# Eight projection matmuls of an attention step, split four and four around the transposes of the probabilities

## The chip, the core and the metric

The kernel runs on one core of a Trainium2 chip. Its engines are TensorE (PE in the rows; its weight loads are listed apart as PEld), VectorE (DVE), ScalarE (ACT), GpSimd (POOL) and SyncE (SP). Each works through its own list of instructions, and they wait for each other on semaphores. The metric is the device time of one execution in microseconds (us); lower is better.

## What is computed

A decoder of two layers on x of 8 batches by 100 tokens by 512. The change lies in one stage of it, the grouped attention with cross attention of layer 0, cut here to what matters:

```
q  = _ln(fp8_linear(ln_out, wq))        # 16 heads of 128, in 8 groups of 2 heads
k, v = _ln(fp8_linear(ln_out, wk)), fp8_linear(ln_out, wv)     # 8 groups of 128
core = _gqa(q, k, v)                    # softmax(q k^T * scale) v, 100 x 100 per head
qx = _ln(fp8_linear(ln_out, wqx))       # a second set of queries
kx, vx = split(cond @ w_kv_x.T)         # cond: 361 rows of context per batch
xout = _gqa(qx, _ln(kx), vx)            # 100 x 361 per head
catq = _div_clamp_fp8(concatenate([core, xout]), proj_smooth)
return einsum('bsi,oi->bso', catq, wproj) * (proj_in_scale * proj_w_scale)
```

The last line is the output projection, from 4096 features to 512.

## The kernel before, in words

The program is a row of stages. The function `grouped_attention` is the one that the change touches. It runs 64 steps, one for each of 8 groups g (outer loop) and 8 batches b (inner loop), numbered n = 8g + b. One step does, for its group and batch, the projections of tokens and context and their norms, and it does the softmax and the weighing of the values for the step before it, n-1. So work of two neighbouring steps overlaps. Nothing reorders anything: each engine runs its instructions in the order in which the function for that engine writes them, and a wait on a semaphore holds all that stands behind it on that engine.

On TensorE a step is, in this order:

- `project_tokens` (L822): 48 matmuls of 100 x 256 or 100 x 128, in bf16 (weights in three parts).
- `scores(n-1)` (L858, L859): scores of the two heads into banks 6 and 7.
- `project_context` (L836): keys and values of the context, 12 matmuls in the program and 24 instructions in the profile, since each f32 matmul there shows as two.
- `turn_probs(n-1)` (L867, L870): waits for `prob_ready`, the normalised probabilities, and transposes them in eight matmuls against the identity. The last one raises `pt_mm`.
- `project_out` (L893), from step 6 on: eight matmuls of 128 x 400 (four rows j by the high and the low part of the weights), all added up in bank 4. They belong to an older unit, six steps back, and their inputs have long been made. The last one raises `proj_mm`.
- `weigh_values(n-1)` (L877, L879): waits for the copies `pT` of the transposed probabilities, then four matmuls in the program.
- `turn(n)` (L845, L849): transposes of the normed context keys `nrm_x` (waits for `ctx_nrm`) and token heads `nrm_t` (waits for `tok_nrm`).

The transposed probabilities are copied out of banks 6 and 7 by two engines: ScalarE (L956, after `pt_mm`) and VectorE (L1099, L1100). On ScalarE the next instructions are the square root for the norms (L994, `sd`), two copies of values (L995, L997) and the normed keys (L1000, `nrm_x`). On VectorE, behind the two copies, come the reciprocal (L1069) that needs that square root, two small operations (L1071, L1073) and the five normed heads (L1076, `nrm_t`). The softmax before it is L1082 to L1085 (maxima) on VectorE, L946 and L948 (exponentials) on ScalarE, and L1089 to L1093 (division) on VectorE.

Of the kernel before, what the change touches and what calls it, by code (L numbers as in the profile page):

```python
# [715 lines left out]
def grouped_attention(nc, core, a, xq, w_raw, w3, kv_raw, o_raw, yf, abs_sums, tern, last_rows_saved):  # L716
# [16 lines left out]
    with ExitStack() as ctx:  # L733
        def sb(name, shape, dt=F32):
# [20 lines left out]
        S_ = {n: core.sem(f"qa_{n}") for n in (  # L755
            "measured",
            "w_in", "kv_in", "o_in", "sm_in", "scales",
            "w_scaled", "w_hi", "w_rest", "w_mid", "w_lo", "o_hi", "o_lo", "rsm_ready",
            "ctx_mm", "tok_mm", "tok_st", "tok_mv", "ctx_st", "stats_ready", "sd_ready", "recip_done",
            "rs_ready", "tok_rs", "ctx_nrm", "tok_nrm", "tt_mm", "tt_out", "tx_mm", "tx_out",  # L760
            "s_mm", "max_done", "nm_ready", "exp_done", "rsum_ready", "prob_ready", "pt_mm",
            "pt_out_act", "pt_out_dve", "o_mm", "o_read", "y_clip", "y_exp", "y_magic", "y_sum",
            "catq_ready", "proj_mm", "proj_out")}
# [7 lines left out]
        def early(n, than):  # L771

            return n < than
# [35 lines left out]
        def _(pe):  # L809
            ident = core.ident  # L810

            def project_tokens(g, s, b, n):

                if b == 0 and not early(g, 1):
                    pe.wait_ge(S_["w_lo"], g * C)
                if not early(n, 1):
                    pe.wait_ge(S_["tok_nrm"], n)
                at = 0
                for kind, width in enumerate(KIND_COLS):
                    for part in range(3):  # L820
                        for k in range(C):
                            mm = pe.matmul(psum[0:T, 2 + at // 512, at % 512:at % 512 + width],  # L822
                                           xq[:, kind, k, b * T:(b + 1) * T], w3[:, s, part, k, at:at + width],
                                           start=(part == 0 and k == 0), stop=(part == 2 and k == C - 1))
                    at += width
                mm.then_inc(S_["tok_mm"], 1)

            def project_context(g, s, b, n):

                if b == 0:  # L830
                    pe.wait_ge(S_["kv_in"], g * 16 + 16)
                if not early(n, 1):
                    pe.wait_ge(S_["ctx_nrm"], n)
                for i, (t0, rows) in enumerate(TILES):
                    for k in range(C):
                        mm = pe.matmul(psum[0:rows, i // 2, (i % 2) * 256:(i % 2) * 256 + 256],  # L836
                                       ctxT[:, k, b * TC + t0:b * TC + t0 + rows], kv_raw[:, s, k, :],
                                       start=(k == 0), stop=(k == C - 1))
                mm.then_inc(S_["ctx_mm"], 1)

            def turn(n):

                pe.wait_ge(S_["ctx_nrm"], n + 1)
                for i, (t0, rows) in enumerate(TILES):
                    mm = pe.transpose(psum[:, 5, t0:t0 + rows], nrm_x[0:rows, i, :], ident[0:rows, 0:rows])  # L845
                mm.then_inc(S_["tx_mm"], 1)
                pe.wait_ge(S_["tok_nrm"], n + 1)
                for i in range(5):
                    mm = pe.transpose(psum[:, 7, i * T:(i + 1) * T], nrm_t[:, i, :], ident[0:T, 0:T])  # L849
                mm.then_inc(S_["tt_mm"], 1)  # L850

            def scores(n):
                pe.wait_ge(S_["tt_out"], n + 1)
                pe.wait_ge(S_["tx_out"], n + 1)
                if not early(n, 1):
                    pe.wait_ge(S_["o_read"], n)
                for h in range(2):
                    pe.matmul(psum[0:T, 6 + h, 0:TC], qT[:, 2 + h, :], kxT[:, :], start=True, stop=True)  # L858
                    mm = pe.matmul(psum[0:T, 6 + h, TC:TC + T], qT[:, h, :], kT[:, :], start=True, stop=True)  # L859
                mm.then_inc(S_["s_mm"], 1)  # L860

            def turn_probs(n):
                pe.wait_ge(S_["prob_ready"], n + 1)
                for i, (t0, rows) in enumerate(TILES):
                    for h in range(2):
                        at = (2 * i + h) % 4
                        pe.transpose(psum[0:rows, 6 + i // 2, at * T:(at + 1) * T],  # L867
                                     prob[:, h, t0:t0 + rows], ident[0:T, 0:T])
                for h in range(2):
                    mm = pe.transpose(psum[0:T, 7, (2 + h) * T:(3 + h) * T], prob[:, h, TC:TC + T],  # L870
                                      ident[0:T, 0:T])
                mm.then_inc(S_["pt_mm"], 1)

            def weigh_values(b, n):
                pe.wait_ge(S_["pt_out_act"], n + 1)
                pe.wait_ge(S_["pt_out_dve"], n + 1)
                pe.matmul(psum[:, 6, 0:2 * T], v[:, b % 2, :], pT[0:T, 6:8, :], start=True, stop=True)  # L877
                for i, (t0, rows) in enumerate(TILES):
                    mm = pe.matmul(psum[:, 6, 2 * T:4 * T], vx[0:rows, b % 2, i, :], pT[0:rows, 2 * i:2 * i + 2, :],  # L879
                                   start=(i == 0), stop=(i == 2))  # L880
                mm.then_inc(S_["o_mm"], 1)

            def project_out(g, quad, c, u, bank=4):

                if quad == 0:
                    pe.wait_ge(S_["o_lo"], g * 4 + c + 1)
                if c == 0:
                    pe.wait_ge(S_["catq_ready"], u + 4)
                if not early(u, 1) and bank == 4:
                    pe.wait_ge(S_["proj_out"], u)  # L890
                for j in range(4):
                    for part in range(2):
                        mm = pe.matmul(psum[:, bank, 0:HALF], o2[:, part, j, c * P:(c + 1) * P], catq[quad][:, j, :],  # L893
                                       start=(part == 0 and j == 0), stop=(part == 1 and j == 3))
                mm.then_inc(S_["proj_mm"], 1)

            def step(g, s, b, n):
                project_tokens(g, s, b, n)
                if not early(n, 1):
                    scores(n - 1)  # L900
                project_context(g, s, b, n)
                if not early(n, 1):
                    turn_probs(n - 1)
                if not early(n, OUT_LAG):
                    project_out(*out_chunk(g, b, n))
                if not early(n, 1):
                    weigh_values((b - 1) % 2, n - 1)
                turn(n)

            steps(step)  # L910
            last = G * B - 1
            scores(last)
            project_out(G - 1, 0, 2, last - 5)
            project_out(G - 1, 0, 3, last - 4, 2)
            turn_probs(last)
            weigh_values((B - 1) % 2, last)
# [3 lines left out]
            for i in range(2):  # L920
                mm = pe.matmul(psum[:, 4, i:i + 1], core.ones[:, :], core.total[:, i:i + 1], start=True, stop=True)
# [306 lines left out]
OUT_LAG = 6  # L1228
# [3 lines left out]
def out_chunk(g, b, n):  # L1232

    c = (b + 2) % 4
    if b < 2:
        return g - 1, 0, c, n - OUT_LAG
    if b < OUT_LAG:
        return g - 1, 1, c, n - OUT_LAG
    return g, 0, c, n - OUT_LAG
# [1817 lines left out]
```

## Time and profile before

| | |
|---|---|
| device time, median of 3 runs | 2172.48 us (2171.51 to 2521.76) |
| span of the profiled execution | 2167.6 us |
| lowest run less that span | 3.9 us |
| median less that span | 4.9 us |
| mean granted TensorE clock | 0.997 |
| TensorE busy, share of the span | 97% |
| VectorE, ScalarE, GpSimd busy | 69%, 54%, 22% |

The span goes from the first to the last instruction of one profiled execution. That execution's own device time is not given apart; what lies around the span is taken as the 4.9 us by which the median of the runs exceeds it. The third of the runs, 2521.76 us, stands far off the other two. The busy shares are averages over stages with different limits.

### The profile page before, as it was taken

The page shows a single profiled execution, that of the slowest core. Times are in us where ns is not written, and L with a number is a line of the kernel's source. Part 1 is how long each engine was busy: PE and PEld are TensorE (multiplying, and loading weights), DVE is VectorE, ACT ScalarE, POOL GpSimd, SP SyncE. Part 2 cuts the span into 40 slices and gives each one's busy share as a digit, 9 for nine tenths or more (in the row PEclk, how much of TensorE's full clock was granted, in tenths as well). Part 3 has the DMA queues.
Part 4 walks back from the last instruction along what each step waited for, and adds up shares of the span by engine and source line. Part 5 has one row for each costly group of instructions (what it writes and reads, how often), then busy time and mean ns, then how long its engine had stood idle before and what let it go on. Part 6 is the DMA issues. An engine that isn't in the chain of part 4 may idle for free. (4 is left out here: it accounts for less than half of the span.)

```text
span 2167.6 us, 35343 instructions
## 1 busy us (share of the span) xinstructions
PE 2100.4 (97%) x13176; PEld 1660.6 (77%) x13176; DVE 1500.8 (69%) x4041; ACT 1178.3 (54%) x3019; POOL 476.0 (22%) x439
## 2 busy tenths in 40 slices
PE   9998999999999999999998899999999999998998
PEld 5645788888888888888887797656656785665997
DVE  2496768777777777777666865676676757885555
ACT  2163767576766767576655444435535446773332
POOL 1210222222222221212111000253243100122442
PEclk9999999999999999999999999999999999999999
DMA  7023110111111100110100403143231320001300
GB/s 259 8 73 115 37 40 9 40 39 38 40 37 40 37 29 20 40 38 11 57 11 1 168 3 110 54 153 117 81 117 59 147 96 21 2 2 73 146 1 31
DMA packets 44178, 130.08 MB, mean 60 GB/s; under 512 B 6711, under 2 KB 21847, under 8 KB 40039
## 3 DMA queue, kind: packets, MB, share of 16 engines
q1 hardware_dynamic: 32488, 108.32, 13.7%
q10 hardware_dynamic: 9504, 8.50, 1.3%
q0 software_dynamic: 2016, 11.01, 1.3%
q8 instruction: 104, 1.70, 0.3%
q14 instruction: 66, 0.54, 0.1%
HBM read 108.05 MB, written 19.37 MB: 59 GB/s over the span
## 5 line engine op out<-in xcount | busy, mean ns | idle before, releaser
L836 PE MATMUL psum<-la_w_both,context 128*128 128x256 f32 (+1 forms) x1536 | 343.7, 380 | 0.2 <-DMA la_w_both<-in_qa_kv 0.2
L836 PEld LDWEIGHTS psum<-la_w_both,context 128*128 128x128 f32 (+1 forms) x1536 | 277.2, 184 | 45.4 <-DMA la_w_both<-in_qa_kv 0.5
L822 PE MATMUL psum<-qa_w,room 128*100 128x256 bf16 (+1 forms) x3072 | 264.0, 246 | 2.3 <-PEq L60 2.3
L822 PEld LDWEIGHTS psum<-qa_w,room 128*100 128x100 bf16 x3072 | 253.1, 125 | 3.2 <-issue 3.2
L946 ACT ACTIVATE qa_prob<-psum,qa_nm 100x361 f32<-100x361 f32 x128 | 71.9, 562 | 165.6 <-DVE qa_nm L1085 165.5
L1196 POOL TENSOR_TENSOR qa_w<-qa_w_raw,qa_w 128x768 bf16<-128x768 f32 x28 | 46.1, 1645 | 362.7 <-DVE qa_w L1027 362.7
L2742 ACT ACTIVATE it_prob<-psum,it_nm 100x257 f32<-100x257 f32 (+1 forms) x256 | 101.9, 412 | 40.0 <-DVE it_nm L2773 40.0
L1047 DVE BATCH_NORM_STATS2 qa_st<-psum 100x6 f32<-100x128 f32 x320 | 69.6, 284 | 74.1 <-PE psum L822 73.9
L1202 POOL TENSOR_TENSOR qa_o<-la_w_qt,qa_o 128x512 fp32r<-128x512 f32 x32 | 40.6, 1269 | 350.5 <-DVE qa_o L1035 350.5
L1076 DVE TENSOR_SCALAR qa_nrm_t<-psum,qa_mv,qa_sd 100x128 f32<-100x128 f32 x320 | 107.8, 403 | 2.4
L858 PE MATMUL psum<-qa_kxT,qa_qT 128*100 128x361 f32 x256 | 98.8, 468 | 1.3 <-ACT qa_qT L940 1.3
L1089 DVE RECIPROCAL qa_rsum<-qa_sums 100x4 f32<-100x4 f32 x64 | 11.4, 178 | 125.3 <-ACT qa_prob L948 125.3
L946 ACT ACT_TABLE_LOAD x64 | 82.1, 1283 | 24.9 <-ACT qa_size L979 13.4
L1541 PE MATMUL psum<-gf_parts,gf_w 128*128 128x400 f32 x480 | 93.0, 346 | 0.0
L2027 PE MATMUL psum<-X,la_w_q 128*128 128x400 f32 x256 | 89.9, 499 | 0.0
L1984 PE MATMUL psum<-la_oT,la_w_vo 128*128 128x400 f32 x256 | 89.5, 500 | 0.0
L1541 PEld LDWEIGHTS psum<-gf_parts,gf_w 128*128 128x128 f32 x480 | 87.8, 188 | 0.6 <-issue 0.3
L1208 POOL TENSOR_TENSOR qa_yt<-qa_yb,qa_ym 128x400 f32<-128x400 bf16 x64 | 60.2, 941 | 114.4 <-DVE qa_ym L1118 114.4
L952 ACT ACT_TABLE_LOAD x64 | 82.1, 1283 | 1.1
L1000 ACT ACTIVATE qa_nrm_x<-psum,qa_nmr,qa_sd 128x128 f32<-128x128 f32 (+1 forms) x192 | 74.0, 454 | 9.6 <-DVE qa_nmr L1071 3.1
L2027 PEld LDWEIGHTS psum<-X,la_w_q 128*128 128x128 f32 x256 | 48.6, 190 | 36.5 <-issue 1.9
L879 PE MATMUL psum<-qa_pT,qa_vx 128*128 128x200 f32 (+1 forms) x384 | 75.6, 332 | 0.0
(376 smaller groups left out, 5062.3 us busy)
## 6 DMA issues: line engine op xcount, KB each, us to landing
qa_w_raw<-in_qa_w SPq DMA_DIRECT2D x8, 1536.0 KB, 6.5
la_gf_raw<-in_gf_w SPq DMA_DIRECT2D x16, 768.0 KB, 4.9
qa_piece<-in_tf_pieces ACTq DMA_DIRECT2D x64, 128.0 KB, 2.1
la_w_qt<-in_qa_o SPq DMA_DIRECT2D x8, 1024.0 KB
context<-in_context SPq DMA_DIRECT2D x8, 722.0 KB, 12.4
gf_ternary<-la_gf_made POOLq DMA_DIRECT2D x7, 768.0 KB
gf_ternary<-keep POOLq DMA_DIRECT2D x7, 768.0 KB
tf_ring<-in_tf_w SPq DMA_DIRECT2D x10, 512.0 KB, 3.5
```

The costliest lines, as they stand in the source:

```text
L822: mm = pe.matmul(psum[0:T, 2 + at // 512, at % 512:at % 512 + width], xq[:, kind, k, b * T:(b + 1) * T], w3[:, s, part, k, at:at + width], ...
L836: mm = pe.matmul(psum[0:rows, i // 2, (i % 2) * 256:(i % 2) * 256 + 256], ctxT[:, k, b * TC + t0:b * TC + t0 + rows], kv_raw[:, s, k, :], ...
L858: pe.matmul(psum[0:T, 6 + h, 0:TC], qT[:, 2 + h, :], kxT[:, :], start=True, stop=True)
L879: mm = pe.matmul(psum[:, 6, 2 * T:4 * T], vx[0:rows, b % 2, i, :], pT[0:rows, 2 * i:2 * i + 2, :], start=(i == 0), stop=(i == 2))
L946: act.activation(prob[:, h, 0:TC], psum[0:T, 6 + h, 0:TC], ACT.Exp, scale=QK_SCALE, bias=nm[:, h:h + 1], accum_out=sums[:, h:h + 1])
L952: act.activation(spare[:, :], core.eps[1.0], ACT.Sqrt)
L1000: last = act.activation(nrm_x[0:rows, i, :], psum[0:rows, i // 2, (i % 2) * 256:(i % 2) * 256 + P], ACT.Identity, scale=sd[0:rows, i:i + 1 ...
L1076: last = dve.tensor_scalar(nrm_t[:, i, :], psum[0:T, bank, c0:c0 + P], mv[0:T, 3 + i, 0:1], sd[0:T, 3 + i:4 + i], ALU.subtract, ALU.mult)
L1541: mm = pe.matmul(hidden_bank(m, u), weights(j)[:, u, k * P:(k + 1) * P], parts[:, part, k, half_of(half)], start=(part == 0 and k == 0), s ...
L1984: mm = pe.matmul(psum[:, 7 - i % 2, 0:HALF], w_vo[:, j, c * P:(c + 1) * P], oT[:, j, cols(h)], start=(j == 0), stop=(j == 3))
L2027: mm = pe.matmul(psum[:, bank, 0:HALF], (w_q if kind == "q" else w_rot)[:, k, i * P:(i + 1) * P], X[:, k, cols(h)], start=(k == 0), stop=( ...
L2742: last = act.activation(prob[:, r, j, x0:x1], psum[0:T, 2 * r + j, x0:x1], ACT.Exp, scale=IT_SCALE, bias=nm[:, r, at:at + 1], accum_out=su ...
```

## The change

`project_out` gets a list of the rows j that it does. A step calls it twice: rows 0 and 1 (four matmuls, with the waits that stood at its head) ahead of `turn_probs`, and rows 2 and 3 (four matmuls, the last of which raises `proj_mm`) where all eight stood. The eight still add up in bank 4 in the same order; the eight transposes, which write banks 6 and 7, now stand in the middle of them. Nothing is added, removed or resized, and the calls behind the loop still do all eight at once.

```diff
-            def project_out(g, quad, c, u, bank=4):
-
-                if quad == 0:
+            def project_out(g, quad, c, u, bank=4, rows=(0, 1, 2, 3)):
+
+                if rows[0] == 0 and quad == 0:
                     pe.wait_ge(S_["o_lo"], g * 4 + c + 1)
-                if c == 0:
+                if rows[0] == 0 and c == 0:
                     pe.wait_ge(S_["catq_ready"], u + 4)
-                if not early(u, 1) and bank == 4:
+                if rows[0] == 0 and not early(u, 1) and bank == 4:
                     pe.wait_ge(S_["proj_out"], u)
-                for j in range(4):
+                for j in rows:
                     for part in range(2):
                         mm = pe.matmul(psum[:, bank, 0:HALF], o2[:, part, j, c * P:(c + 1) * P], catq[quad][:, j, :],
                                        start=(part == 0 and j == 0), stop=(part == 1 and j == 3))
-                mm.then_inc(S_["proj_mm"], 1)
+                if rows[-1] == 3:
+                    mm.then_inc(S_["proj_mm"], 1)
...
                 project_context(g, s, b, n)
+                if not early(n, OUT_LAG):
+                    project_out(*out_chunk(g, b, n), rows=(0, 1))
                 if not early(n, 1):
                     turn_probs(n - 1)
                 if not early(n, OUT_LAG):
-                    project_out(*out_chunk(g, b, n))
+                    project_out(*out_chunk(g, b, n), rows=(2, 3))
```

TensorE, in the first step that has a projection (n = 6), in the kernel before, from the context's projection to the turn of the heads:

```order
L836 MATMUL psum<-la_w_both,context 128x256 x8
L836 MATMUL psum<-la_w_both,context 105x256 x4
L867 MATMUL psum<-ident,qa_prob 128x100 x4
L867 MATMUL psum<-ident,qa_prob 105x100 x2
L870 MATMUL psum<-ident,qa_prob 100x100 x2
L893 MATMUL psum<-qa_catq,qa_o 128x400 x8
L877 MATMUL psum<-qa_pT,qa_v 128x200
L879 MATMUL psum<-qa_pT,qa_vx 128x200 x3
L845 MATMUL psum<-ident,qa_nrm_x 128x128 x2
L845 MATMUL psum<-ident,qa_nrm_x 128x105
L849 MATMUL psum<-ident,qa_nrm_t 128x100 x5
```

And in the changed kernel at the same place:

```order
L836 MATMUL psum<-la_w_both,context 128x256 x8
L836 MATMUL psum<-la_w_both,context 105x256 x4
L893 MATMUL psum<-qa_catq,qa_o 128x400 x4
L867 MATMUL psum<-ident,qa_prob 128x100 x4
L867 MATMUL psum<-ident,qa_prob 105x100 x2
L870 MATMUL psum<-ident,qa_prob 100x100 x2
L893 MATMUL psum<-qa_catq,qa_o 128x400 x4
L877 MATMUL psum<-qa_pT,qa_v 128x200
L879 MATMUL psum<-qa_pT,qa_vx 128x200 x3
L845 MATMUL psum<-ident,qa_nrm_x 128x128 x2
L845 MATMUL psum<-ident,qa_nrm_x 128x105
L849 MATMUL psum<-ident,qa_nrm_t 128x100 x5
```

Four of the eight L893 now stand between the context's projection and the transposes of the probabilities, and four between these and the weighing of the values (L877). All 58 steps from n = 6 on change in this way.

ScalarE, in a step of the changed kernel, from the copy of the transposed probabilities on (the numbers of its lines are three higher than before):

```order
L959 ACTIVATE qa_pT<-psum 128x400
L997 ACTIVATE qa_sd<-qa_mv,consts 128x8
L998 ACTIVATE qa_vx<-psum 128x256
L1000 ACTIVATE qa_vx<-psum 105x128
L1003 ACTIVATE qa_nrm_x<-psum,qa_nmr,qa_sd 128x128 x2
L1003 ACTIVATE qa_nrm_x<-psum,qa_nmr,qa_sd 105x128
```

Its order is that of the kernel before, and so are those of VectorE, GpSimd and SyncE: the square root for the norms (L994 before, L997 now) stands right behind the copy `qa_pT` (L956 before, L959 now).

## Rows read from the trace of the kernel before

**Rows 1.** the page of the kernel before, its part 1

```profile
PE 2100.4 (97%) x13176; PEld 1660.6 (77%) x13176; DVE 1500.8 (69%) x4041; ACT 1178.3 (54%) x3019; POOL 476.0 (22%) x439
```

**Rows 2.** three stretches: busy us (x instructions) by engine, granted clock, DMA share, GB/s

```profile
295.00:1145.00 850.00, 845.76 (x6196) 749.09 (x6195) 633.47 (x2358) 572.05 (x1450) 177.46 (x161) 1.00 0.10 33
1145.00:1177.00 32.00, 30.04 (x221) 26.51 (x220) 21.08 (x84) 17.86 (x48) 6.31 (x6) 1.00 0.00 1
1799.70:1803.00 3.30, 3.16 (x5) 1.85 (x6) 3.09 (x8) 3.15 (x10) 0.00 (x0) 0.50 0.51 164
```

**Rows 3.** TensorE's matmuls in order of time, one step: start, busy us, count

```profile
591.83 4.13 PE L822 MATMUL psum<-qa_w,room 128*100 128x256 bf16 x48
...
597.36 5.37 PE L836 MATMUL psum<-la_w_both,context 128*128 128x256 f32 x24
602.56 0.69 PE L867 MATMUL psum<-ident,qa_prob 100*128 100x100 f32 x6
...
603.21 1.71 PE L893 MATMUL psum<-keep,qa_o 128*128 128x400 f32 x8
604.76 0.50 PE L877 MATMUL psum<-qa_pT,qa_v 100*128 100x200 f32 x2
...
607.18 0.39 PE L822 MATMUL psum<-qa_w,room 128*100 128x256 bf16 x2
```

**Rows 4.** the last six of that step's projection matmuls

```profile
603.66 1.26 PE L893 MATMUL psum<-keep,qa_o 128*128 128x400 f32 x6
```

**Rows 5.** TensorE's weight loads, same step

```profile
602.36 0.73 PEld L867 LDWEIGHTS psum<-ident,qa_prob 100*128 100x128 f32 x6
...
604.59 0.36 PEld L877 LDWEIGHTS psum<-qa_pT,qa_v 100*128 100x128 f32 x2
...
606.08 0.31 PEld L845 LDWEIGHTS psum<-ident,qa_nrm_x 128*128 128x128 f32 x3
606.69 0.46 PEld L849 LDWEIGHTS psum<-ident,qa_nrm_t 100*128 100x128 f32 x5 [0.30 <-DVE qa_nrm_t L1076]
```

**Rows 6.** VectorE, the same step

```profile
602.04 0.27 DVE L1093 TENSOR_SCALAR qa_prob<-qa_prob,qa_rsum 100x100 f32<-100x100 f32 x1
...
603.64 0.31 DVE L1064 BATCH_NORM_AGGREGATE qa_mv<-qa_st 128x2 f32<-128x6 f32 x3
603.87 0.34 DVE L1099 COPY qa_pT<-psum 105x200 f32<-105x200 f32 x1
604.12 0.36 DVE L1100 COPY qa_pT<-psum 100x200 f32<-100x200 f32 x1
604.39 0.19 DVE L1069 RECIPROCAL qa_sd<-qa_sd 128x8 f32<-128x8 f32 x1
...
604.95 1.69 DVE L1076 TENSOR_SCALAR qa_nrm_t<-psum,qa_mv,qa_sd 100x128 f32<-100x128 f32 x5
```

**Rows 7.** ScalarE, same step

```profile
603.47 0.51 ACT L956 ACTIVATE qa_pT<-psum 128x400 f32<-128x400 f32 x1 [0.98 <-PE psum L870]
603.99 0.30 ACT L994 ACTIVATE qa_sd<-qa_mv,consts 128x8 f32<-128x8 f32 x1
...
604.88 1.16 ACT L1000 ACTIVATE qa_nrm_x<-psum,qa_nmr,qa_sd 128x128 f32<-128x128 f32 x3
```

**Rows 8.** waits of the weight loads, 290 to 1180 us: total, times, longest

```profile
PEld psum L849 <- DVE qa_nrm_t L1076: 16.5, 56, 0.3
PEld psum L867 <- DVE qa_prob L1093: 2.8, 2, 1.4
...
PEld psum L877 <- issue: 1.2, 4, 0.3
```

**Rows 9.** line 893, 290 to 1180 us: durations in ns, first and last start

```profile
L893 PE MATMUL psum<-qa_catq,qa_o x240: 338/343/431, 296.1 to 1175.3; 128*128 128x400 f32 x120
...
L893 PE MATMUL psum<-keep,qa_o x224: 340/345/430, 357.5 to 1142.4; 128*128 128x400 f32 x112
```

**Rows 10.** TensorE in the last step of the loop

```profile
1173.27 0.75 PE L867 MATMUL psum<-ident,qa_prob 100*128 100x100 f32 x6 [0.98 <-DVE qa_prob L1093]
```

## Prediction

> **What bounds the kernel now.** I read the page first [rows 1]: TensorE is busy for 97% of the span, and the next engine for 69%. A share that high can hide short waits, since the end of a matmul is modelled and two neighbours overlap in the rows. So the table of stretches comes next [rows 2]: from 295 to 1145 us, the bulk of the loop that is changed, TensorE is busy for 845.76 of 850 us at a clock of 1.00. Then one step in order of time [rows 3]. Its first matmul starts at 591.83 and that of the next step at 607.18, so a step is 15.35 us. What matters is where TensorE stands still in it, and the weight loads show that best [rows 5], since they are not modelled. Three places are to be compared with the engine that releases them.
>
> First, the transposes of the probabilities (L867). Their load starts at 602.36, 0.05 us after the last division L1093 ends (602.04 + 0.27 = 602.31) [rows 5, 6]. So TensorE does meet that wait, but it costs nothing: the 24 matmuls before start every (602.56 - 597.36) / 24 = 0.217 us, the same as inside their row, (5.37 - 0.38) / 23 = 0.217 with 0.38 for one matmul [rows 3]. The probabilities come just as TensorE gets there.
>
> Second, the values (L877). Their load starts at 604.59, 0.11 after the VectorE copy L1100 ends at 604.48 [rows 5, 6]. That costs nothing either: matmul L877 starts in the rhythm of the ones before it.
>
> Third, the heads (L849). Their load stands idle for 0.30 us and starts at 606.69, 0.05 after the five L1076 end (604.95 + 1.69 = 606.64) [rows 5, 6]. The table of waits has this 56 times, 16.5 us in all [rows 8], so in nearly every step. This wait is real, and the end of a step hangs on it: the next step's first matmul follows right behind.
>
> What sets L1076? Followed back: L1069 (604.39), released by the square root L994 on ScalarE (603.99 + 0.30), which stands right behind the copy L956 (603.47 + 0.51 = 603.98), which waited 0.98 us for the last transpose L870 [rows 6, 7]. So from the transposes of the probabilities to the end of the step there is one chain over three engines, 606.69 - 603.47 = 3.22 us long, with no slack in it. The eight projection matmuls of 343 ns each (overlapped) lie beside it, as cover: TensorE has work for all of it but the last 0.30.
>
> **The change part by part.** Removed and added: nothing. Moved: four of the eight matmuls L893 of a step. Their rhythm: from the third, at 603.66, to L877 at 604.76 there are six, so 1.10 / 6 = 0.183 us each [rows 3, 4]. Four of them are 0.73 us.
>
> Ahead of the transposes they put 0.73 us of work where there was no idle time to fill, so L867 and with it `pt_mm` come 0.73 us later. The wait for the probabilities gains 0.73 of slack, which pays for nothing, since its cost was nothing. Behind the transposes they take 0.73 us of cover from a chain that had none to spare:
>
> - ScalarE: the copy L956 starts at 603.47 + 0.73 = 604.20 and ends at 604.71. L994 can't pass it; it starts at 604.72 instead of 603.99.
> - VectorE: L1064 ended at 603.95 and does not move; the copies then wait for the transposes and start at 604.20 instead of 603.87 (L1099), 0.33 later, ending at 604.81. L1069 waits for the square root and moves by the full 0.73; so L1076 ends at 607.37.
> - TensorE: it reaches L877 at the same time as now, since its own work is the same. There it waits 0.33 for the copies. The load of L845 then waits for ScalarE's L1000, which ends at 606.04 + 0.73 = 606.77. The load of L849 starts at 607.42 instead of 606.69.
>
> The waits at L877 and L845 are parts of the same delay and are not added up: the step ends when L849 is released, 0.73 us later. Nothing behind it gives this back: VectorE and ScalarE do the rest of the step at the same distance behind TensorE as before, only they have more time. The waits at the head of `project_out` (`o_lo`, `catq_ready`, `proj_out`) are for things of earlier steps; no row shows L893 waiting in the loop. `proj_mm` is raised at TensorE's same point, so GpSimd's and VectorE's waits for it do not move. No DMA is moved, and no queue is passed.
>
> How often: 240 + 224 = 464 matmuls L893 in the loop [rows 9], 58 steps of eight. In two of them the probabilities do hold TensorE, 2.8 us together, the table says [rows 8]; the last step is one, with 0.98 us on the matmul side [rows 10]. There the four matmuls fill idle time, `pt_mm` does not move and the step costs nothing more. It saves nothing either, as its end hangs on the same chain. That leaves 56 steps x 0.73 = 40.9 us. Against it: four steps have a halt of up to 0.3 us, 1.2 together, at L877 that no engine causes [rows 8]; if it recurs it falls inside the new wait of 0.33 there. I take 0.9 off for that: 40.0 us.
>
> The price that no row shows is that of the second switch between 400-column matmuls and transposes. The switch that is there: from the first L893 at 603.21 to L877 at 604.76 it is 1.55 us for eight, against 8 x 0.183 = 1.46, so up to 0.09 us a switch; but part of that is the modelled start of the first. Below nothing it can't be, as a step must still load the same weights. I take 0, by the switch from L893 to L877, which keeps the rhythm, and keep 0.09 x 56 = 5.0 us for the range.
>
> Sum: span 2167.6 + 40.0 = 2207.6 us, with the 4.9 around it 2212.5 us, which against the median of 2172.48 is 1.8% slower.
>
> **The rivals.** *Only the copies count.* Someone who looks for the wait that replaces the cover finds L877: 0.33 us a step, 58 x 0.33 = 19 us, 2191.6 us. It would hold if the square root were free of the copy. Against it: L994 stands behind L956 in ScalarE's order, and starts 0.01 us after its end. For it: L1064, which L994 also waits for, ends at 603.95, so the rows before can't tell which of the two releases it.
>
> *The wait that is filled pays for it (not slower).* The mechanism is the wait at L867: had TensorE to stand there for the probabilities, the four matmuls would fill it. The decisive point is a wait of 0.73 us a step: with that, the sum is zero and the time 2172.5 us; in the two last steps there is one of that size [rows 8, 10]. Against it: the rhythm of 0.217 us up to L867 leaves less than 0.01 us, and the load of L867 has no wait in the table but those two.
>
> *The switch costs more.* With 0.09 us for one more switch in a step it is 2212.5 + 5.0 = 2217.5 us, and with two, one on each side of the first four, 2222.5 us. That is the case which passes 2%.
>
> *The clock falls.* TensorE's idle time in a step grows from 0.30 to about 1.03 us. From 1799.70 to 1803.00 the granted clock was 0.50, that is 1.2 GHz; if each of 56 steps lost one such stretch, it would cost 3.3 / 2 x 56 = 92 us, 2305 us. Against it: in the stretch of the last two steps TensorE is busy for 30.04 of 32 us, with waits of 1 us and more, and the clock stays at 1.00 [rows 2]. The changed loop would be busy for about 95%, as much as that stretch.
> The Trainium skill, "TensorE: Matmul & The Clock Gate", in "A second HAM failure mode: psum-queue depth-cycling", tells of a kernel whose short idle times between groups of matmuls let the clock swing between its two levels. By that rule the change would pay the 92 us; by the row of the last two steps it pays none, and the sum goes by the row.
>
> **How the numbers follow.** The chain and its 0.73 us: 0.72, with a time of 2208 to 2216 for the spread of the runs and small switch costs. Only the copies: 0.08. Filled wait: 0.05. Dearer switch: 0.12. Clock: 0.03. The predicted time is 2212.5 us. The range of 2202 to 2222 takes in the likeliest case and the dearer switch, 0.84, and leaves out the others. About 2% is what a measurement of this kernel can tell from no change; that is 2215.9 us, close above the forecast. Slower by more than 2%: the dearer switch, the clock and the upper edge of the likeliest case, 0.22. Faster by more than 2% has no mechanism here: 0.01. Within 2%: 0.77.
>
> **What the changed profile would show.** The step grows from 15.35 to 16.08 us. The weight load of L849 (its line three higher or not, it is the load of `qa_nrm_t`) waits for VectorE 56 times with the longest total, and its wait and those at `qa_nrm_x` and `qa_pT` together come to some 1.03 us a step. ScalarE's copy `qa_pT` starts 0.73 later against the last context matmul, and the square root right behind it. The load of L867 starts about 0.8 us after the division ends, not 0.05. The clock stays at 1.00. If the step grows by 0.33, the square root was not held by the copy; if the first matmul of either half starts more than 0.25 us behind its forerunner, the switch was undercounted; if it does not grow, the probabilities had held TensorE after all.

## The result

The changed kernel is slower: 2201.22 us, median of four runs (2199.28 to 2203.5), against 2174.83 us for the kernel before, now of four. The ratio, which leaves out the slow run of 2521.76 us, is 1.0123, with a 95% interval from 1.0108 to 1.0138, so 24 to 30 us. Forecast were 2212.5 us, 1.8% more, with a range from 2202. The direction and the place are as forecast; the cost is about two thirds of it by the ratio, and the time lies just below the range.

The profiled execution of the changed kernel has a span of 2201.7 us, 34.1 us more than that of before. The tables of stretches, cut at the seventh step (n = 6, the first with a projection) and at the last, tell how much of that is the change. First the changed kernel, then the kernel before; the columns are busy us and instructions of PE, PEld, DVE, ACT and POOL, then granted clock, DMA share and GB/s.

```profile
0.00:290.06 290.06, 270.50 (x1145) 173.46 (x1146) 176.54 (x388) 120.27 (x252) 45.70 (x50) 0.98 0.26 93
290.06:1196.06 906.00, 894.83 (x6386) 769.43 (x6385) 662.03 (x2421) 580.37 (x1489) 183.41 (x167) 1.00 0.09 31
1196.06:2201.70 1005.64, 966.20 (x5650) 721.82 (x5648) 674.38 (x1235) 470.35 (x1280) 246.34 (x223) 0.99 0.20 74
```

```profile
0.00:284.76 284.76, 264.67 (x1144) 168.42 (x1145) 176.29 (x388) 120.34 (x252) 45.75 (x50) 1.00 0.27 94
284.76:1161.40 876.64, 871.42 (x6387) 771.71 (x6386) 650.25 (x2421) 587.15 (x1489) 183.64 (x167) 1.00 0.10 32
1161.40:2167.60 1006.20, 964.27 (x5650) 720.44 (x5648) 674.29 (x1234) 470.86 (x1280) 246.58 (x223) 0.99 0.20 74
```

The loop grew from 876.64 to 906.00 us, by 29.4 us, which lies inside the interval of the runs. The stretch ahead of it, where nothing was changed, is 5.3 us longer at a granted clock of 0.98 against 1.00. It belongs to the one execution and not to the change: in the traces of the ten experiments below the seventh step starts between 284.0 and 288.0 us, and in the two that also split four and four and leave ScalarE's order alone, at 286.7 and 284.0. Behind the loop the two agree to 0.6 us.

### The profile page after: what moved, and what is told of

It is laid out like the page before. It is cut to its first block and busy times, and to the rows that moved or that the text cites. A ratio compares the mean times of both kernels' runs of the same rounds, so it can differ in the third digit from the quotient of the medians.

```text
span 2201.7 us, 35343 instructions
## 1 busy us (share of the span) xinstructions
PE 2131.5 (97%) x13176; PEld 1664.7 (76%) x13176; DVE 1512.9 (69%) x4041; ACT 1171.0 (53%) x3019; POOL 475.4 (22%) x439
## 5 line engine op out<-in xcount | busy, mean ns | idle before, releaser
L836 PE MATMUL psum<-la_w_both,context 128*128 128x256 f32 (+1 forms) x1536 | 343.6, 380 | 0.0
L836 PEld LDWEIGHTS psum<-la_w_both,context 128*128 128x128 f32 (+1 forms) x1536 | 277.2, 184 | 44.9
L1079 DVE TENSOR_SCALAR qa_nrm_t<-psum,qa_mv,qa_sd 100x128 f32<-100x128 f32 x320 | 107.9, 404 | 2.4
L959 ACT ACTIVATE qa_pT<-psum 128x400 f32<-128x400 f32 x64 | 32.3, 505 | 103.0 <-PE psum L870 103.0
L1003 ACT ACTIVATE qa_nrm_x<-psum,qa_nmr,qa_sd 128x128 f32<-128x128 f32 (+1 forms) x192 | 73.9, 454 | 6.0 <-DVE qa_nmr L1074 0.8
```

The lines of the kernel that those rows point to most:

```text
L1003: last = act.activation(nrm_x[0:rows, i, :], psum[0:rows, i // 2, (i % 2) * 256:(i % 2) * 256 + P], ACT.Identity, scale=sd[0:rows, i:i + 1 ...
L1079: last = dve.tensor_scalar(nrm_t[:, i, :], psum[0:T, bank, c0:c0 + P], mv[0:T, 3 + i, 0:1], sd[0:T, 3 + i:4 + i], ALU.subtract, ALU.mult)
```

## The changed kernel's profile

TensorE in order of time, one step (n = 26, the one of [rows 3]):

```profile
607.77 4.13 PE L822 MATMUL psum<-qa_w,room 128*100 128x256 bf16 x48
...
613.30 5.37 PE L836 MATMUL psum<-la_w_both,context 128*128 128x256 f32 x24
618.32 1.08 PE L893 MATMUL psum<-keep,qa_o 128*128 128x400 f32 x4
619.24 0.69 PE L867 MATMUL psum<-ident,qa_prob 100*128 100x100 f32 x6
...
619.88 0.98 PE L893 MATMUL psum<-keep,qa_o 128*128 128x400 f32 x4
620.93 0.58 PE L877 MATMUL psum<-qa_pT,qa_v 100*128 100x200 f32 x2
...
622.57 0.53 PE L845 MATMUL psum<-ident,qa_nrm_x 128*128 128x128 f32 x3
623.18 0.65 PE L849 MATMUL psum<-ident,qa_nrm_t 100*128 100x100 f32 x5
623.66 0.49 PE L822 MATMUL psum<-qa_w,room 128*100 128x256 bf16 x3
```

The step is 623.66 - 607.77 = 15.89 us, where it was 15.35 [rows 3]: 0.55 more, not 0.73. The four matmuls ahead cost what was forecast: L867 starts (619.24 - 613.30) - (602.56 - 597.36) = 0.74 us later, measured from the first context matmul. No switch costs anything: the 24 context matmuls take 24 x 0.217 = 5.21 of the 5.94 us up to L867, which leaves 0.73 for the four L893. Behind the transposes TensorE stands before L877: from 619.88 to 620.93 it is 1.05 us, where four matmuls need 0.73. At L849 the delay has shrunk to 0.55. So 0.19 us was given back between the transposes and the end of the step. The division ends at 618.25 (below), 0.99 ahead of L867, where it was 0.25 [rows 3, 6]: the slack that pays for nothing.

Who kept the weight loads waiting, 290 to 1195 us (total, times, longest):

```profile
PEld psum L877 <- ACT qa_pT L959: 21.3, 57, 0.4
PEld psum L845 <- ACT qa_nrm_x L1003: 20.2, 57, 0.4
PEld psum L849 <- DVE qa_nrm_t L1079: 16.6, 56, 0.3
```

In [rows 8] the heads L849 were the only steady wait, 16.5 us. They still are there with 16.6 us; new are the values (L877) and the context keys (L845), 21.3 and 20.2 us, 57 times each. The table counts idle time of the weight loads, which is not what the matmuls lose: the three waits come to 58.1 us, where the loop grew by 29.4. The four halts without a cause at L877 are gone from it, as forecast.

ScalarE and VectorE at the end of that step:

```profile
620.14 0.51 ACT L959 ACTIVATE qa_pT<-psum 128x400 f32<-128x400 f32 x1 [1.71 <-PE psum L870]
620.54 0.29 ACT L997 ACTIVATE qa_sd<-qa_mv,consts 128x8 f32<-128x8 f32 x1
...
621.36 1.15 ACT L1003 ACTIVATE qa_nrm_x<-psum,qa_nmr,qa_sd 128x128 f32<-128x128 f32 x3
```

```profile
617.98 0.27 DVE L1096 TENSOR_SCALAR qa_prob<-qa_prob,qa_rsum 100x100 f32<-100x100 f32 x1
...
619.59 0.31 DVE L1067 BATCH_NORM_AGGREGATE qa_mv<-qa_st 128x2 f32<-128x6 f32 x3
620.14 0.37 DVE L1102 COPY qa_pT<-psum 105x200 f32<-105x200 f32 x1 [0.25 <-PE psum L870]
620.42 0.36 DVE L1103 COPY qa_pT<-psum 100x200 f32<-100x200 f32 x1
620.86 0.20 DVE L1072 RECIPROCAL qa_sd<-qa_sd 128x8 f32<-128x8 f32 x1
...
621.43 1.69 DVE L1079 TENSOR_SCALAR qa_nrm_t<-psum,qa_mv,qa_sd 100x128 f32<-100x128 f32 x5
```

This is where the 0.19 us are. Measured from the first context matmul of the step (597.36 before, 613.30 now), the copy on ScalarE comes 0.73 us later than before, the square root 0.61 and the reciprocal 0.53. So a part was given back at the square root and a part at the reciprocal.

ScalarE's copy starts at 620.14 and the square root (now L997) 0.40 us behind it, though the copy is busy for 0.51. Before, it was 0.52 us behind [rows 7]: what had held it then was not the copy but the context statistics (L1064), which ended at 603.95, 0.04 before it [rows 6]. Now these end at 619.90, long before. ScalarE's keys (L1003) end at 622.51 and the transposes L845 start at 622.57; the heads (L1079) end at 623.12 and L849 starts at 623.18. The reciprocal (now L1072) starts 0.72 us behind the start of ScalarE's copy, where it was 604.39 - 603.47 = 0.92 [rows 6, 7].

## The experiments

Two theories were put against each other. A was made from the trace of the changed kernel, so the split of four and four can't test it; the other runs can. **A, two arms**: the end of a step waits for the later of two chains of work, called arms here. One arm starts with the transposes of the probabilities (copy and square root on ScalarE, or the copies on VectorE). The other is VectorE's own queue, which starts with the context statistics, after the last L836, and runs over L1064, L1099 and L1100 to the reciprocal L1069. Before the change the second leads by 0.19 us. **B**, the prediction's: one chain from the transposes, without slack.

The step below is the median distance between the first matmuls of neighbouring steps, from n = 6 on, in one trace of each kernel. But for the halts at L877 the steps of a trace agree to about 0.02 us, so a step tells more than a ratio does.

| run | ratio to before, 95% interval | step, us |
|---|---|---|
| before | 1 | 15.34 |
| one ahead, seven behind | 0.9998 [0.999, 1.0007] | 15.35 |
| two ahead, six behind | 1.0034 [1.0022, 1.0045] | 15.52 |
| four ahead, four behind (the change) | 1.0123 [1.0108, 1.0138] | 15.89 |
| six ahead, two behind | 1.0219 [1.0205, 1.0232] | 16.25 |
| before, L1062 early | 0.9962 [0.9947, 0.9977] | 15.23 |
| before, L1062 in the idle time | 0.9955 [0.994, 0.9969] | 15.20 |
| the change, L1062 in the idle time | 1.0122 [1.0108, 1.0137] | 15.88 |
| the change, root ahead of the copy | 1.0083 [1.0069, 1.0098] | 15.71 |
| before, a wait per head | 0.9906 [0.9888, 0.9925] | 15.05 |
| before, both | 0.9899 [0.9885, 0.9914] | 15.02 |
| the change, a wait per head | 1.0059 [1.0039, 1.0079] | 15.59 |

### How many ahead: one, two, six

The calls in `step`, against those of the changed kernel, with the eight matmuls numbered 0 to 7 (here one ahead; 2 and 6 in the other two runs):

```diff
-                    project_out(*out_chunk(g, b, n), rows=(0, 1))
+                    project_out(*out_chunk(g, b, n), part_of=range(1))
...
-                    project_out(*out_chunk(g, b, n), rows=(2, 3))
+                    project_out(*out_chunk(g, b, n), part_of=range(1, 8))
```

> Of the eight projection matmuls of a step only the first is ahead of the transposes of the probabilities, seven behind. The transposes then come 0.18 us later in each of 56 steps. Theory A (two arms): the end of a step is set by the later of two arms, the chain from the transposes (copy, square root, reciprocal, heads) and VectorE's own queue from the context statistics on, and in the kernel before the second leads by 0.19 us; so 0.18 us costs nothing: ratio to before 1.000, step 15.34 us. Theory B (the prediction's, one arm without slack): 56 x 0.18 = 10.2 us, ratio 1.0047, step 15.52 us.

> Two of the eight projection matmuls ahead of the transposes, six behind: the transposes come 0.37 us later. Theory A (two arms, 0.19 us of slack): 0.18 us a step, 10 us, ratio 1.0046, step 15.52 us. Theory B (no slack): 20.5 us, ratio 1.0094, step 15.71 us.

> Six of the eight projection matmuls ahead of the transposes, two behind: the transposes come 1.10 us later. Theory A: 1.10 - 0.19 = 0.91 us a step, 51 us, ratio 1.0235, step 16.25 us. Theory B: 1.10 us a step, 61.5 us, ratio 1.028, step 16.44 us. A third theory C, that a part of any delay is given back (0.55 of 0.73, so three quarters stay): 0.82 us a step, 46 us, ratio 1.021, step 16.16 us.

Each matmul ahead moves the transposes by 0.18 us, and the steps grow by 0.00, 0.18, 0.55 and 0.91 us for one, two, four and six of them. For two, four and six that is the delay less 0.19 us; one stays just below 0.19 and is free, where B wanted 0.18 us a step and a ratio of 1.0047, outside the interval. C, a share given back, is out by its step of 16.16 us for six; its ratio of 1.021 would fit.

A's own ratios for two and six, 1.0046 and 1.0235, lie just outside the measured intervals. They left out the four halts at L877 [rows 8], which all or in part fall inside the delay. In the traces the loops are 9.3 and 49.7 us longer than that of before, ratios of 1.0043 and 1.0229, and these lie inside.

With one ahead VectorE and ScalarE stand like this at the end of a step:

```profile
606.96 0.30 DVE L1067 BATCH_NORM_AGGREGATE qa_mv<-qa_st 128x2 f32<-128x6 f32 x3
...
607.44 0.35 DVE L1103 COPY qa_pT<-psum 100x200 f32<-100x200 f32 x1
607.71 0.19 DVE L1072 RECIPROCAL qa_sd<-qa_sd 128x8 f32<-128x8 f32 x1
```

```profile
606.97 0.51 ACT L959 ACTIVATE qa_pT<-psum 128x400 f32<-128x400 f32 x1 [1.16 <-PE psum L870]
607.37 0.29 ACT L997 ACTIVATE qa_sd<-qa_mv,consts 128x8 f32<-128x8 f32 x1
```

The square root L997 follows the copy L959 by 0.40, as in the changed kernel. Yet the reciprocal L1072 still stands 0.27 us behind VectorE's second copy (607.71 - 607.44), exactly as before (604.39 - 604.12 [rows 6]): VectorE's own queue still sets it, and the transposes' arm has become 0.18 us later at no cost. It has all but caught up: the reciprocal starts 0.74 us behind ScalarE's copy, and 0.72 is what the transposes' arm needs, as the changed kernel shows.

### VectorE's arm made shorter, TensorE untouched

```diff
+                dve.wait_ge(S_["tok_mv"], n + 1)
+                dve.tensor_tensor(mv[0:T, 3:8, 1], mv[0:T, 3:8, 1], wsc2[0:T, :], ALU.mult).then_inc(S_["stats_ready"], 1)
                 dve.wait_ge(S_["ctx_mm"], n + 1)
...
-                dve.wait_ge(S_["tok_mv"], n + 1)
                 dve.wait_ge(S_["ctx_st"], n * 3 + 3)
-                dve.tensor_tensor(mv[0:T, 3:8, 1], mv[0:T, 3:8, 1], wsc2[0:T, :], ALU.mult).then_inc(S_["stats_ready"], 1)
```

This is the second of the two edits; in the first the two added lines stand at the end of `token_stats`, ahead of the maxima.

> The kernel before, with one small VectorE operation (the product of the token variances and wsc2, L1062) moved from behind the context statistics L1057 to the end of the token statistics; nothing else. TensorE's order is untouched. Theory A: VectorE's queue from the context statistics on leads, so its end comes 0.08 to 0.15 us earlier in each of 63 steps: 5 to 9 us faster, ratio 0.996 to 0.998, step 15.19 to 15.26 us. Theory B (the transposes' chain leads): no change, step 15.34 us.

> The kernel before, with the same small operation L1062 moved only as far as VectorE's idle time ahead of the context statistics, so behind the probabilities and not ahead of them. TensorE's order is untouched. Theory A (two arms): VectorE's arm gets 0.15 us shorter or more, the other arm takes over 0.19 below, and nothing delays the probabilities: 0.15 to 0.19 us a step over 61 steps, 9 to 11.5 us faster, ratio 0.9947 to 0.996, step 15.16 to 15.20 us. Theory B (the transposes' chain alone): no change.

Both are faster, by 0.11 and 0.14 us a step, without a change on TensorE; B is out. The gain in the second is a little under A's 0.15 to 0.19. The end of the step in the second, VectorE and then ScalarE's copy:

```profile
602.03 0.15 DVE L1056 TENSOR_TENSOR qa_mv<-qa_mv,qa_wsc 100x5 f32<-100x5 f32 x1
...
603.78 0.36 DVE L1100 COPY qa_pT<-psum 100x200 f32<-100x200 f32 x1
604.05 0.19 DVE L1069 RECIPROCAL qa_sd<-qa_sd 128x8 f32<-128x8 f32 x1
```

```profile
603.27 0.51 ACT L956 ACTIVATE qa_pT<-psum 128x400 f32<-128x400 f32 x1 [0.98 <-PE psum L870]
```

L1056 is the moved product. The reciprocal comes 0.27 behind the second copy again and 604.05 - 603.27 = 0.78 us behind ScalarE's copy, where it was 0.92 [rows 6, 7]; that is the gain. The 0.72 that the other arm needs is not reached, so VectorE's arm still leads.

In the first edit the operation stands ahead of the softmax and delays it, and the waits show it (290 to 1160 us):

```profile
PEld psum L867 <- DVE qa_prob L1093: 17.4, 57, 1.6
PEld psum L849 <- DVE qa_nrm_t L1076: 0.2, 1, 0.2
```

The steady wait at the heads is gone from the table, but the probabilities, which cost nothing before, now hold TensorE's weight loads 57 times. ScalarE's copy comes 0.08 us later in a step than before, and the reciprocal follows it by 0.72 (medians over the loop): here the transposes' arm has become the later one, without any split. The same operation, moved as far as the idle time only, does not pay that. The ratios of the two edits, 0.9962 and 0.9955, don't tell them apart; their steps, 15.23 and 15.20 us, do.

### The same edit in the changed kernel

> The changed kernel (four ahead, four behind) with L1062 moved into the same idle time. Theory A: with four ahead the transposes' arm leads by 0.55 us, so a shorter VectorE arm is worth nothing: as the changed kernel, step 15.89 us, ratio to before 1.0125. If VectorE's queue as such sets the end of a step, 0.19 us a step come back: 15.70 us, ratio 1.007.

The step is 15.88 us and the ratio 1.0122, against 15.89 and 1.0123 for the change alone: the edit is worth nothing here. The same edit is worth 0.14 us where VectorE's arm leads and nothing where it does not. This pair shows the two arms most plainly.

### The square root ahead of the copy, in the changed kernel

```diff
                 if not early(n, 1):
                     exps(n - 1)
-                    probs_out(n - 1)
                 act.wait_ge(S_["stats_ready"], n * 2 + 2)
                 act.activation(sd[:, :], mv[:, :, 1], ACT.Sqrt, bias=core.eps[1e-5]).then_inc(S_["sd_ready"], 1)
+                if not early(n, 1):
+                    probs_out(n - 1)
```

> The changed kernel with ScalarE's square root of the norms put ahead of the copy of the transposed probabilities, which it then no longer waits behind. Theory A: in the changed kernel the transposes' arm goes through copy and root (root 0.40 us after the copy starts, reciprocal 0.72 after); with the root out of it the reciprocal follows VectorE's second copy, some 0.56 us after: 0.17 us less a step, 15.72 us, ratio to before 1.0095 to 1.010. The prediction's reading, with the two copies alone counting, expects 0.33 us a step over before: 15.67 us, ratio 1.0085. If neither copy nor root is in the chain: 15.89 us, ratio 1.0125.

The step is 15.71 us, 0.18 less than in the changed kernel; the copy and the root behind it were in its chain. ScalarE and VectorE now:

```profile
614.02 0.30 ACT L996 ACTIVATE qa_sd<-qa_mv,consts 128x8 f32<-128x8 f32 x1 [1.50 <-DVE qa_mv L1068]
614.23 0.51 ACT L959 ACTIVATE qa_pT<-psum 128x400 f32<-128x400 f32 x1
```

```profile
614.51 0.36 DVE L1104 COPY qa_pT<-psum 100x200 f32<-100x200 f32 x1
614.78 0.19 DVE L1073 RECIPROCAL qa_sd<-qa_sd 128x8 f32<-128x8 f32 x1
```

The root L996 starts ahead of the copy L959, and the reciprocal L1073 follows the second VectorE copy by 0.27 us again. The ratio, 1.0083, can't tell the two numbers for this case apart (1.0095 to 1.010, and 1.0085); the step lies nearer to A's 15.72 than to 15.67, but both only say that the arm then goes over VectorE's copies.

### A wait for each head

```diff
-                pe.wait_ge(S_["tok_nrm"], n + 1)
                 for i in range(5):
+                    pe.wait_ge(S_["tok_nrm"], 5 * n + i + 1)
                     mm = pe.transpose(psum[:, 7, i * T:(i + 1) * T], nrm_t[:, i, :], ident[0:T, 0:T])
```

VectorE raises `tok_nrm` behind each of the five L1076, and the next step's wait counts to 5n.

> The kernel before, with a semaphore increment behind each of the five normed heads L1076 and a wait ahead of each of their five transposes L849, instead of one for all five. The end of a step then hangs on the last head alone or on TensorE's own work: up to 0.27 us less a step. In the steps with b below 4 VectorE has only 0.16 us to spare before it needs the next token projection, so some 0.1 us comes back as a wait for the probabilities there: 0.1 us in half of the steps and 0.27 in the other half, 11 us, ratio 0.995, between 0.992 and 0.998. If the end of a step did not hang on the heads, 1.000.

It is faster by more than was expected: 0.29 us in steps of every b, with a ratio of 0.9906, below the 0.992 to 0.998 on record. The waits, 290 to 1160 us:

```profile
PEld psum L867 <- DVE qa_prob L1092: 2.8, 2, 1.4
PEld psum L877 <- issue: 1.2, 4, 0.3
PEld psum L845 <- ACT qa_nrm_x L1000: 0.7, 4, 0.2
```

The steady wait for the heads is gone and no other came; what is left in the table stood in that of the kernel before too. The expected relapse for b below 4 did not come. It rested on a wait of 0.16 us on VectorE before it takes the next token projection, read as all that it had to spare. The row that waits started 0.42 us behind the start of its forerunner (L1118) in the step of [rows 3]; here, without a wait, it starts 0.18 us behind. So 0.24 us was to spare and not 0.16, by the same error as in the prediction: the end of a row was taken for the moment at which the next can start. No run was made on this alone.

> The kernel before with both edits: a wait per head, and L1062 in VectorE's idle time. With a wait per head alone TensorE had no wait left in a step (15.05 us), so the second edit has nothing to shorten but 0.03 us ahead of the key transposes: step 15.02 to 15.05 us, ratio 0.9895 to 0.991. If the two gains added up, 0.29 + 0.14 = 0.43 us a step: 14.91 us, ratio 0.9865.

The step is 15.02 us and the ratio 0.9899: the two gains do not add up. The second edit shortens a wait that the first had made harmless. This is the best version found, about 21 us faster than the kernel before (2151.42 against 2172.52 us in this comparison), though its interval overlaps that of the wait per head alone.

> The changed kernel (four ahead, four behind) with a wait per head. Theory A, carried one wait further: the heads no longer set the end of the step; the wait for ScalarE's normed keys (L1000 before the transposes L845) does, 2.43 us after the copy starts, and TensorE then needs 0.8 us for its eight transposes. Against the kernel before 0.25 us a step more: step 15.6 us, ratio 1.005 to 1.007. If the delay were all at the heads, the split would be free with this wait: step 15.05 to 15.1 us, ratio 0.991.

The step is 15.59 us and the ratio 1.0059, as A had it. The waits, 290 to 1160 us:

```profile
PEld psum L877 <- ACT qa_pT L959: 21.0, 56, 0.4
PEld psum L845 <- ACT qa_nrm_x L1003: 19.9, 56, 0.4
```

The heads are out of the table, and the split still costs, since ScalarE's normed keys come late by the same cause. Against the wait per head without the split (15.05) the split costs 0.54 us a step, nearly the 0.55 that it costs without it.

## Why the prediction was wrong in its size

- **TensorE has no idle time in front of the transposes, so four matmuls there cost 4 x 0.183 us.** Right: L867 came 0.74 later in the step shown, 0.73 in the median of the loop.
- **Behind the transposes cover is missing, and the waits at L877 and L845 are parts of the one delay.** Right in kind: both waits came, and the end of the step hangs on L849. Of the signs, the three waits together were forecast at 1.03 us a step and came to 1.02; with a delay that was 0.19 too large, that agreement is luck. L849 was to have the longest total and has the shortest of the three.
- **"So from the transposes of the probabilities to the end of the step there is one chain over three engines ... with no slack in it."** This is the step that failed. The chain had 0.19 us of slack. The splits of two, four and six measure it, the split of one bears it out, and the runs with L1062 in the idle time, alone and in the changed kernel, show what led instead: VectorE's queue from the context statistics on. So the term "56 steps x 0.73 = 40.9 us" was too large: measured are 56 x 0.545 = 30.5 us. Less the four halts, which took 1.1 us together in the kernel before, that is the 29.4 us by which the loop grew.
- **The reason for the error: the busy time of a row was read as the time until its successor can start.** "ScalarE: the copy L956 starts at 603.47 + 0.73 = 604.20 and ends at 604.71. L994 can't pass it; it starts at 604.72": measured is a start 0.40 us behind the copy's. That the root stood 0.01 behind the copy's end was chance. The Trainium skill bears on this, in "Perfetto Trace Analysis", section "Optimizing Scalar/DVE Operations": it says of the fixed data-access cost of a ScalarE or VectorE operation that the profiled latency is about twice the time that the engine is busy, since the half for the write acknowledgement overlaps with the next instruction. These rows agree in kind, with a start-to-start of 0.40 for a row of 0.51; the factor of two was not tested here. The rows of the kernel before had it: L1069 starts at 604.39, while L1100 ahead of it is busy until 604.48 [rows 6], so the reciprocal was not held by the root (free from 604.29) but stood in VectorE's rhythm. The rival *only the copies count* named the right doubt, that "the rows before can't tell which of the two releases it", but priced it as all or nothing, 0.33 or 0.73 us a step.
- **Two steps cost nothing, and four halts fall inside the new wait.** Right: from the first matmul of step 62 to that of step 63 it is 16.35 us in both kernels, the stretch from step 63 on is no longer than before, and no halt is left in the table.
- **The clock.** It stayed at 1.00 through the loop, with three waits in each step. TensorE was busy for 894.83 of its 906.00 us, so 99% and not the 95% of the prediction, which counted 1.03 us a step as idle, from waits of the weight loads. The rule of the Trainium skill, "TensorE: Matmul & The Clock Gate", in "A second HAM failure mode: psum-queue depth-cycling", did not show here; the 0.98 in the profiled execution lies ahead of the loop.
- **The switch.** Right: 0.00 us in all four splits, where the first transpose comes 0.18, 0.37, 0.73 and 1.10 us later, as the matmuls alone make it.
- **The 4.9 us around the span.** In every run whose span is on record the time is only 1.7 to 1.8 us above the span. By that the profiled execution of the kernel before took some 2169.4 us, and the other 3.1 of the 4.9 are its distance from the median. The sum is not hurt, since it goes from that execution to the median of the runs either way.

What stays open: what the four halts of up to 0.3 us at L877 are. With one ahead, and with a wait per head, they fall into the same four steps as before the change, and no run was made on them.

## What to carry to other kernels

Before work is taken from behind a producer as cover, follow every arm that the next wait hangs on, back to where they part, and compare start with start: here the difference between the two arms was free, and the rest was paid in full. Where an engine waits for the last of a row of equal results, a semaphore step for each of them can take the wait away altogether; here that was worth 0.9%, three quarters of what the split cost. And a small operation is better moved into a gap of its engine than past the work that feeds the bound engine; here that made 0.03 us a step.

## What was unexpected of the hardware

On ScalarE the activation behind a copy of 128 x 400 started 0.40 us after the copy's start, whose row is 0.505 us long; on VectorE the reciprocal behind a copy of 100 x 200 started 0.27 us after, with a row of 0.36. The weight load of the heads' transposes (L849) started 0.05 us after the row of the last head had ended, in each of the nine kernels that wait for all five heads at once.
